# Edge steps of a graph network: old state read by the transposing load alone and turned back by TensorE, the second layer's bias seeded by ScalarE, four gathers per group without a pause

## The reference, cut to what matters

```python
edge_attr = swish(edge_attr_raw @ enc_W + enc_b)
for _ in range(4):
    e_in = concat([edge_attr, x[src], x[dst]])
    e_upd = layernorm(swish(e_in @ eW1 + eb1) @ eW2 + eb2, eg, ebeta)
    edge_attr = edge_attr + e_upd
    agg = segment_sum(edge_attr, dst)
    n_in = concat([x, agg])
    x = x + layernorm(swish(n_in @ nW1 + nb1) @ nW2 + nb2, ng, nbeta)
out = layernorm(x0 + x)
```

## Time and profile before

| what | value |
|---|---|
| time, median of 3 runs | 3196.34 us (3195.55 to 3199.94) |
| span of the profiled execution, first to last instruction | 2909.7 us |
| own time of the profiled execution | not listed apart; median less span is 286.6 us |
| busy: PE, DVE, ACT, POOL | 2323.9, 2307.0, 1691.7, 1680.3 us |
| mean granted TensorE clock | 0.938 of full speed |
| DMA | 850,391 packets, 680.36 MB, mean 234 GB/s |

### The profile page before, as it was taken

One profiled execution on the slowest core, in us unless ns is written; L12 is line 12 of the kernel. 1 busy time (PEld: TensorE's weight loads), 2 busy tenths in 40 slices (PEclk: granted clock), 3 DMA queues, 4 the chain that ended last, 5 costly groups with the idle time before them and its releaser, 6 DMA issues.

```text
span 2909.7 us, 78888 instructions
## 1 busy us (share of the span) xinstructions
PE 2323.9 (80%) x24950; PEld 1743.3 (60%) x24950; DVE 2307.0 (79%) x6778; ACT 1691.7 (58%) x5167; POOL 1680.3 (58%) x1679
## 2 busy tenths in 40 slices
PE   2666678788788787888888788887788789989895
PEld 1333566666666466666766466666566467777774
DVE  6888578877777488788878487887788579999897
ACT  2777456555555465565655465555566366666664
POOL 1444776666660377676761376666663177777760
PEclk9666899999999999999999999999999999999998
DMA  3777999999995699999995699999996599999990
GB/s 112 244 243 246 243 265 264 255 265 246 257 261 143 183 258 268 263 276 276 286 254 151 177 265 260 269 254 260 251 271 185 157 235 257 251 253 255 248 223 23
DMA packets 850391, 680.36 MB, mean 234 GB/s; under 512 B 490079, under 2 KB 699228, under 8 KB 849950
## 3 DMA queue, kind: packets, MB, share of 16 engines
q1 hardware_dynamic: 774702, 469.61, 70.3%
q0 software_dynamic: 75264, 205.62, 25.7%
HBM read 428.62 MB, written 144.35 MB: 197 GB/s over the span
## 4 chain that ended last, share of the span: by engine, by line
PE 44%; DMA 15%; issue 12%; POOL 11%; SPq 8%; DVE 6%; ACT 2%; DVEq 1%; ACTq 0%; POOLq 0%
PE psum L1143 11%; POOL arena L1076 10%; PE psum L1159 9%; PE psum L1132 8%; DMA arena<-node_tables 7%; DMA arena<-node_tables,idx_all 5%; PE psum L1124 4%; PE psum L1177 3%; PE psum L1578 2%; SPq L1033 2%; SPq L1039 2%; PE psum L1617 2%; DMA arena<-attr_p 2%; PE psum L1591 2%; PE psum L1154 1%
## 5 line engine op out<-in xcount | busy, mean ns | idle before, releaser
L1076 POOL DMA_INDIRECT arena<-node_tables,idx_all x1568 | 1559.0, 994 | 972.8 <-issue 398.6
L1245 ACT ACTIVATE arena<-psum 128x1024 f16<-128x1024 f32 x392 | 401.1, 1023 | 922.3 <-PE psum L1143 918.1
L1350 DVE SCALAR_TENSOR_TENSOR arena<-psum,arena 128x1024 f16<-128x1024 f32 x392 | 478.3, 1220 | 414.0 <-ACT psum L1246 348.6
L1159 PE MATMUL psum<-w_hi,arena 128*128 128x128 f16 x6272 | 590.2, 219 | 3.9 <-DVE arena L1350 3.9
L1159 PEld LDWEIGHTS psum<-w_hi,arena 128*128 128x128 f16 x6272 | 549.4, 114 | 53.6 <-DVE arena L1350 6.5
L1159 PE MATMUL psum<-w_lo,arena 128*128 128x128 f16 x3136 | 545.9, 219 | 0.0
L1132 PE MATMUL psum<-ident,arena 128*128 128x128 f16 x6272 | 437.1, 225 | 74.4 <-DMA arena<-node_tables,idx_all 74.0
L1386 DVE SCALAR_TENSOR_TENSOR arena<-arena 128x128 f32<-128x128 f32 x1568 | 490.6, 347 | 4.1 <-DVE arena L290 0.4
L1124 PE MATMUL psum<-arena 128*128 128x256 fp8e4 x1568 | 242.2, 278 | 311.3 <-issue 174.5
L1143 PE MATMUL psum<-arena,w_hi 128*128 128x512 f16 x1568 | 488.8, 395 | 0.0
L1132 PEld LDWEIGHTS psum<-ident,arena 128*128 128x128 f16 x6272 | 396.5, 101 | 105.2 <-DMA arena<-node_tables,idx_all 96.2
(11 more groups left out here) (169 smaller groups left out, 2738.9 us busy)
## 6 DMA issues: line engine op xcount, KB each, us to landing
state<-arena SPq DMA_DIRECT2D x392, 256.0 KB, 3.9
arena<-state SPq DMA_DIRECT2D x392, 256.0 KB
arena<-matrices SPq DMA_DIRECT2D x392, 128.0 KB
arena<-node_tables SPq DMA_DIRECT2D x784, 64.0 KB
node_tables<-arena SPq DMA_DIRECT2D x100, 256.0 KB, 2.4
arena<-node_tables,idx_all POOLq DMA_INDIRECT x1568
arena<-rel_rows SPq DMA_DIRECT2D x98, 128.0 KB, 4.0
matrices<-arena SPq DMA_DIRECT2D x98, 128.0 KB, 3.7
```

Source lines behind the costliest of these rows:

```text
L1076: pool.indirect_dma_start(out=rows[k][:, t, :], out_offset=None, in_=p_table, in_offset=bass.IndirectOffsetOnAxis(ap=idx_all[:, g, t:t + 1 ...
L1159: x = pe.matmul(ps_v(k2)[:, t * P:(t + 1) * P], h[k2][:, half, :].rearrange("c (q t) -> c t q", t=TPG)[:, t, :], w[:, half, :], start=Fals ...
L1245: act.activation(hh[k2], ps_h(k2), ACT.Silu).then_inc(S("hh"), 1)
L1350: dve.scalar_tensor_tensor(hl[k2], ps_h(k2), 1.0, hh[k2], ALU.mult, ALU.subtract).then_inc(S("hl"), 1)
```

## The change

- The order of a group's edges is now t*128 + p. The state in DRAM is laid out as [high or low half][tile][feature], so that every operand that went through a strided view is contiguous.
- In the fast path the plain load of the state (`st_in`, line 1021) is gone. The transposing load fills one of eight buffers and waits for `turned` of n-8. Its source is 128 rows of 1024 halves, where it was 512 rows of 256.
- PE gets `turn_back(n-4)` between `output(n-1)` and `node_sums(n-7)`: eight matmuls against the identity add the old high and low halves, upright again, into bank 6 of PSUM. It waits for `new` of n-5.
- DVE's scaling reads its addend from that bank and so adds both halves at once. `add_old` is gone.
- From the third group of a step on, the bias matmul is gone: ACT copies the float32 bias row, repeated, into the bank (`seed(n)`, after `silu(n)`, waiting for `gu` of n-2), and PE's `output` waits for it.
- On POOL the wait ahead of the third gather is not reached (`HOLD = TPG`).
- In the encoding stage the load of the raw attributes takes 512 pieces of 4 floats where it took 128 of 16. Setup loads and centres one more bias row.

```diff
+RE = 8
+HOLD = TPG
+BIAS_ACT = True
...
-                    sp.dma_start(at_in[k][:, 0:TPG * RAW],
-                                 attr_p[g * GE:(g + 1) * GE, :].rearrange("(p t) w -> p (t w)", t=TPG)).then_inc(S(f"at{k}"), 16)
+                    sp.dma_start(at_in[k][:, 0:TPG * RAW].rearrange("p (t w) -> p t w", t=TPG),
+                                 attr_p[g * GE:(g + 1) * GE, :].rearrange("(t p) w -> p t w", t=TPG)).then_inc(S(f"at{k}"), 16)
...
-                    sp.dma_start(st_in[k8].rearrange("p t c -> p (t c)"), state[g, :, :]).then_inc(S(f"st{k8}"), 16)
...
-                    sp.dma_start(eT[k], state[g, :, :].rearrange("p (t c) -> (p t) c", t=TPG), transpose=True).then_inc(S(f"et{k}"), 16)
...
+                def load_state(n):
+                    if n >= RE:
+                        sp.wait_ge(S("turned"), n - RE + 1)
+                    if n >= G1:
+                        sp.wait_ge(S(f"out{(n - G1) % R}"), 16 * self.ring(n - G1))
+                    sp.dma_start(turned_in[n % RE].rearrange("f k (t e) -> f (k t) e", t=TPG),
+                                 state[n % G1, :, :], transpose=True).then_inc(S(f"st{n % RE}"), 16)
...
+                    for t in range(TPG):
+                        if t == HOLD and n > R:
+                            pool.wait_ge(S("v"), n - R)
...
+                    if BIAS_ACT and n - first >= 2:
+                        pe.wait_ge(S("seed"), n - 2 * s - 1)
+                    else:
+                        if n >= 2:
+                            pe.wait_ge(S("gu"), n - 1)
+                        pe.matmul(ps_v(k2), ones16[:, :], v_bias[:, :], start=True, stop=False, skip_group_check=True)
...
+                def turn_back(n):
...
+                    if n:
+                        pe.wait_ge(S("new"), n)
+                    for t in range(TPG):
+                        for p in range(2):
+                            x = pe.matmul(ps_e[:, t * P:(t + 1) * P], turned_in[n % RE][:, p, t * P:(t + 1) * P], ident16[:, :],
+                                          start=t == 0 and p == 0, stop=p == 1, skip_group_check=True)
+                    x.then_inc(S("turned"), 1)
...
+                def seed(n):
...
+                    act.wait_ge(S("gu"), n - 1)
+                    act.copy(ps_v(n % 2).rearrange("p (t f) -> p t f", t=TPG),
+                             v_row[:, :].unsqueeze(1).to_broadcast([P, TPG, D])).then_inc(S("seed"), 1)
...
+                    if t == 0:
+                        dve.wait_ge(S("newton"), self.newton_base(n) + NEWTON_OPS)
+                        dve.wait_ge(S("gu"), n + 1)
+                        dve.wait_ge(S("turned"), n + 1)
...
+                    x = dve.scalar_tensor_tensor(e_new[k][:, t * P:(t + 1) * P], gu[k][:, t * P:(t + 1) * P],
+                                                 rs[pair][:, m:m + 1], ps_e[:, t * P:(t + 1) * P], ALU.mult, ALU.add)
```

More of the change, by code:

```diff
@@ L140, in build_program @@
         sq = [take(GE) for _ in range(2)]
-        st_in = [take(GE, F16).rearrange("p (t c) -> p t c", t=TPG) for _ in range(R8)]
-        st_out = [take(GE, F16).rearrange("p (t c) -> p t c", t=TPG) for _ in range(R)]
+        st_in = [take(GE, F16).rearrange("p (k e) -> p k e", k=2) for _ in range(R8)]
+        st_out = [take(GE, F16).rearrange("p (k e) -> p k e", k=2) for _ in range(R)]
         gu = [take(GE) for _ in range(R)]
@@ L148, in build_program @@
         q_win = [take(H, F16) for _ in range(R)]
-        eT = [take(GE, F16).rearrange("p (k e) -> p k e", k=2) for _ in range(R)]
+        eT = [take(GE, F16).rearrange("p (k e) -> p k e", k=2) for _ in range(2)]
+        turned_in = st_in
         both = [take(GE // 2) for _ in range(R12)]
@@ L180, in build_program @@
         e0 = [take(GE) for _ in range(R)]
-        st0 = [take(GE, F16).rearrange("p (t c) -> p t c", t=TPG) for _ in range(R)]
+        st0 = [take(GE, F16).rearrange("p (k e) -> p k e", k=2) for _ in range(R)]
         rel_b = [take(GE // 2, F16) for _ in range(R)]
@@ L241, in build_program @@
         ps_t = psum[:, 6, :].bitcast(F16)
+        ps_e = psum[:, 6, :]
         ps_a = psum[:, 7, :]
@@ L1006, in sp @@
                 fence(sp)
[L1008 to L1032, removed]
-                    sp.dma_start(eT[k], state[g, :, :].rearrange("p (t c) -> (p t) c", t=TPG), transpose=True).then_inc(S(f"et{k}"), 16)
[L1034 to L1039, removed]
-                        sp.dma_start(q_win[k][:, h * H:(h + 1) * H],
-                                     q_table.rearrange("n (s e) -> (n s) e", s=2)[ds(w, P), :]).then_inc(S(f"q{k}"), 16)
-                def store(g):
-                    sp.wait_ge(S("el"), c(g))
-                    sp.dma_start(state[g, :, :], st_out[g % R].rearrange("p t c -> p (t c)")).then_inc(S(f"out{g % R}"), 16)
-                for g in range(G1 + LAG + 6):
-                    if g < G1:
-                        if s == 0 or g >= 3:
-                            load_state(g, s)
-                            load_matrices(g, s)
-                    if 0 <= g - LAG - 6 < G1 and s < STEPS - 1:
-                        store(g - LAG - 6)
-                    if g < G1:
-                        load_rows(g)
-                if s < STEPS - 1:
-                    for g in range(3):
-                        load_state(g, s + 1)
-                        load_matrices(g, s + 1)
-                tables_or_result(sp, s)
@@ L1062, in pool @@
             def pool(self, pool, s):
                 S = self.S
-                if s and not self.wide:
-                    for t in range(CH):
-                        pool.wait_ge(ND(f"tab{t}"), 16 * NCH * s)
                 def gather(g):
@@ L1284, in high @@
                             act.wait_ge(S(f"out{k}"), 16 * self.ring(s, i, off - R))
-                    elif not self.wide and s:
-                        act.wait_ge(S(f"out{k}"), 16 * self.ring(s - 1, 0, max(x for x in range(G1) if x % R == k)))
-                    act.copy(st_out[k][:, :, 0:D], e_new[k].rearrange("p (t f) -> p t f", t=TPG)).then_inc(S("eh"), 1)
+                    act.copy(st_out[k][:, 0, :], e_new[k]).then_inc(S("eh"), 1)
                 return silu, turned, squares, high
```

460 lines of the change are left out of this document (334 added, 126 removed).

## The result

The changed kernel takes 3347.57 us (median of 4 runs, 3343.64 to 3356.47) against 3195.95 us before (4 runs, 3194.37 to 3199.94): a ratio of 1.0479, 95% interval 1.0461 to 1.0496. It is slower by 152 us where 158 us less were forecast. The runs were made in batches, each on one chip. In other batches the same kernel before took about 2910 us, and the unchanged change then took 0.928 of that. Ratios compare only executions in the fast state, so they can differ a little from the ratio of the two medians.

What follows compares the result with a forecast made beforehand. The prediction took SP's queue and DMA traffic to bound steps 0 to 2 and POOL's gathers step 3; -198.4 + 15 + 20 + 4 + 1 = -158 us took 3196.3 to 3038 us, range 2998 to 3130 us.

Steps and rivals of the forecast that it cites:

- The 286.6 us between span and median: Difference between traced span and timed median of the kernel before; kept as a constant outside the span, untouched by the change.
- The bound moves from SP to POOL: Edge steps 0 to 2: SP's queue stops binding, POOL's gathers set 5.22 us per group, Silu passes span 505 to 515 us.
- The residue of 15 us: Edge steps 0 to 2: 0.05 us given back in each of 291 intervals for SP's little slack and hiccups.
- Step 3: Last edge step, which stores no state: already bound by POOL's issuing of gathers, 505.3 us, to gain nothing.
- The transposing load: SP's issue of the state load in its new shape: costed at nothing over the 1.25 us of before.
- Rival C: Edge steps: the transposing load costs SP twice as much in its new shape, 3405 us in all; chance 0.07.
- The encoding stage: Attribute load on SP with 512 pieces for 128: +0.19 us per group, 20 us, issue about 0.57 us.
- The node stages: Tails of the steps: more PE work, less DVE work, +1 us per step, 4 us in all.
- The seed: ACT's copy of the bias row in each edge group: 0.60 us, hidden under POOL's pace.
- the 198 us: Edge steps 0 to 2: saving from their falling to the last step's 505.3 us, 198.4 us less.
- The pause removed: POOL's wait ahead of the third gather: taking it away was worth between nothing and a few us, taken as nothing.
- D: Edge steps: new waits between PE, ACT and DVE make a loop of say 5.5 us per group, 3136 us; chance 0.06.

Runs made afterwards that it cites:

- e5: The kernel before, without an edit, on the same chip as the unedited change: 3194.98 us, in a batch where the kernel before had 3199.22 us.
- e0: The kernel before, without an edit, run for a second trace: 2907.24 us beside 2912.07 us.
- e6: The changed kernel, without an edit, a third time: 2713.19 us beside a kernel before of 2916.70 us, ratio 0.9281.
- e12: The changed kernel with POOL's pause ahead of the third gather put back: 3209.96 us beside a kernel before of 3197.33 us, ratio 1.0040.
- e4: The changed kernel, without an edit, run again: 3352.44 us, ratio 1.0470 to the kernel before of its batch.
- e17: The changed kernel without two of each group's four gathers, except in a step's first four groups: 2678.73 us beside a kernel before of 3226.05 us, ratio 0.8314.
- e13: The changed kernel with PE's bias matmul and POOL's pause both put back: 3203.84 us beside a kernel before of 3197.33 us, ratio 1.0017.

## Why the prediction was wrong

**The step that failed** is "The 286.6 us between span and median I keep as they are, since nothing in the change touches what lies around the span". Only 1.7 to 1.8 us lie around a span: 3350.63 against 3348.9 us in the changed kernel, 3194.98 against 3193.2 in e5, 2907.24 against 2905.4 in e0. The trace and the times were of two levels, and the whole argument was read from the one that wasn't being timed. The difference of a tenth between span and median was in the prediction as a number and should have stopped it: not a constant to carry over but the sign that the trace shows another bound.

**The steps at level 2900**, by e6 against e0, whose spans are 2712.3 and 2905.4 us, 193 less where 158 were forecast (changed span 2751). Of the 35 us between, 16 lie in the edge groups, 14 in the encoding stage and 5 in the node stages and the setup; the kernel before itself varies from 2888 to 2952 us in e6's batch, so the sum can't be judged more finely. The first Silu pass and the gathers of step 3 in e6:

```profile
L1526 ACT ACTIVATE arena<-psum x98: 1024/1024/1025, 321.3 to 832.4; 128x1024 f16<-128x1024 f32 x98
L1526 ACT ACTIVATE arena<-psum x98: 1024/1024/1025, 932.4 to 1434.3; 128x1024 f16<-128x1024 f32 x98
L1526 ACT ACTIVATE arena<-psum x98: 1024/1024/1025, 1533.2 to 2036.2; 128x1024 f16<-128x1024 f32 x98
L1526 ACT ACTIVATE arena<-psum x98: 1024/1024/1027, 2136.5 to 2635.9; 128x1024 f16<-128x1024 f32 x98
```

```profile
L1394 POOL DMA_INDIRECT arena<-node_tables,idx_all x392: 942/949/1559, 2125.3 to 2629.3; - x196
```

- The bound moves from SP to POOL: right. 511.1, 501.9, 503.0 and 499.4 us, for 505 to 515 forecast. The gathers of step 3 take 504.0 us, 1.29 us each. PE waits ahead of the gathered rows (25.3 us from 350 to 880 us) and for 6.6 us ahead of the destination matmuls, where the earlier trace rows had 100 us.
- The residue of 15 us that SP was to keep: steps 0 to 2 together take 17.8 us more than three times step 3. The size is right; that SP causes it isn't shown.
- Step 3 was to gain nothing and takes 499.4 us for 504.7 in e0.
- The transposing load: median 1262 ns over all 392 of e6 in its new shape against 1253 in quiet stretches before; from 350 to 880 us it is 1262 too, where before had 1478. Rival C had no ground. The Trainium skill, page "DMA: Bandwidth & Descriptors", section "Latency and other measured facts", has a DMA transpose with a middle dimension that isn't contiguous lose about 30% of its bandwidth. The time of the issue shows no such loss for this shape; the rate of the transfer itself isn't shown here. The prediction made 30% less bandwidth into 30% more time, 0.38 us; 1.25 / 0.7 gives 0.54 us more, an estimate by that page, and neither came.
- The encoding stage: half. The attribute issue has a median of 404 ns, against 382 before, not 570, and the first Silu pass comes 6.4 us later than in e0 (321.3 to 314.9), for 20 forecast. The 0.06 us per 128 pieces taken from line 720 was too dear.
- The node stages: right. From the last Silu pass of a step to the first of the next e6 has 100.0 us after step 0, for 99.2 before.
- The seed: 581 ns on ACT for 600 forecast, hidden.

**At level 3200** two terms were wrong. First, steps 0 to 2 were never bound by SP there (e5: 6.35 us per group in step 0 and 6.40 in step 3), so the 198 us were not to be had: with the pause back, the change is worth +0.4%. Second, "The pause removed is worth nothing [...] Between nothing and a few us I take nothing": putting the pause back takes off 142 us, 93% of the loss (e12 against e4). Its reason, that the gap of POOL is 0.30 us everywhere, holds at level 2900 alone; at level 3200 POOL idles 1.4 us in each group beyond its usual gaps with the pause (e12) and 1.6 us without (e4).

**The rivals.** None held the case. D came nearest in form, a loop of some engine longer than POOL's pace in all four steps, but named PE's new waits, and those hardly showed: `turn_back` (line 1459) waits for 1.1 us in 530. Of the signs of being wrong that the prediction lists, one came: gaps of POOL that end with PE, 676.9 us.

**What stays open.** Shown is that the stops come with the gathers (e17), that the traces have them only at level 3200, and that without the pause PE is idle longer in them (e4, e12). That it is the four gathers in a row that do it is read from two timelines. How a gather holds up PE in the middle of a line isn't shown. Nor is it shown why POOL, with the pause, stops about 1 us ahead of each pair: both semaphores that it waits for were met 2.6 us or more before the gather starts (medians of e12). What makes a batch run at one level or the other is open too; it is not the chip, which was the same for e4 and e6.

## What to carry to other kernels

When the span of the trace and the timed median differ by more than a few us, explain the difference before reading the trace for a bound. Here both levels had to be profiled, and they have different bounds. A wait that seems to do nothing in one trace may be worth much in another: putting it back took 142 us off here. e13, with only the single transposing load and its turning back kept, takes 0.93 to 0.94 of the kernel before at level 2900 and 1.0017 at level 3200, and is what I would keep, while the whole change wins 0.928 or loses 1.047.

## What was not expected of the hardware

- The same program has two levels, 2881 to 2953 us and 3192 to 3228 us, each throughout a batch, and one chip had both. The granted clock of the kernel before was 0.92 to 0.94 at the faster level and 0.94 to 0.95 at the slower one, so it isn't the clock.
- PE can stand still for about 0.6 to 0.7 us, from one start to the next, between two matmuls of one line that nothing in the program separates. The changed kernel has 161 such waits in 530 us at line 1422; e17, with half of the gathers, has none there.
- A cost that is not in proportion: half of the gathers took away nearly all of the stops, and 670 us with them.
